# Layer 0's inverse roots of the first groups: from GpSimd's power operation to VectorE's Newton steps

## What is computed

```python
h = layernorm(x) * (1 + ca) + sa
x = x + ga * attn(h)         # attn ends: out = (out - mu) * rsqrt(var + EPS) * ln_w + ln_b; u * out @ Wout.T + bout
h = layernorm(x) * (1 + cb) + sb
# expert layer: two of 8 experts for each token, in the order of the tokens, at most 640 tokens for each expert
gate_logits = xt @ Wg + bg;  top_v, top_i = top_k(gate_logits, 2)
expert_label = one_hot(top_i, E).sum(axis=1)
seq = cumsum(expert_label, axis=0) * expert_label      # the place of a token in its expert's queue
flat_idx = where((seq > 0) & (seq <= capacity), e * capacity + seq - 1, E * capacity)
buf = zeros((E * capacity + 1, d)).at[flat_idx.reshape(-1)].set(src)
```

## Time and profile before

| | us |
|---|---|
| median of 3 runs | 839.18 (839.06 to 839.41) |
| the profiled execution | 838.07 |
| its span, first to last instruction | 836.7 |
| PE busy | 799.2 (96%) |
| DVE busy | 604.1 (72%) |
| ACT busy | 434.5 (52%) |
| POOL busy | 395.0 (47%) |
| chain that ended last | PE 72%, POOL 9%, DVE 6%, issue 5%, DMA 4%, ACT 3% |

### The profile page before, as it was taken

One profiled execution on the slowest core, in us unless ns is written; L12 is line 12 of the kernel. 1 busy time (PEld: TensorE's weight loads), 2 busy tenths in 40 slices (PEclk: granted clock), 3 DMA queues, 4 the chain that ended last, 5 costly groups with the idle time before them and its releaser, 6 DMA issues.

```text
span 836.7 us, 32664 instructions
## 1 busy us (share of the span) xinstructions
PE 799.2 (96%) x13828; PEld 699.4 (84%) x13828; DVE 604.1 (72%) x1779; ACT 434.5 (52%) x942; POOL 395.0 (47%) x399
## 2 busy tenths in 40 slices
PE   6999987899998899999999999999999999989998
PEld 5777767799997688888888888888898889878887
DVE  7898887567545766675777776786867777768865
ACT  6556634344544746566566565575665654523322
POOL 4348887425454735643646646447443434400000
PEclk9999999999999999999999999999999999999999
DMA  9814141233413000000100000200000000048751
GB/s 282 285 45 181 41 134 26 76 94 116 131 48 110 27 3 4 28 4 4 53 4 4 29 4 3 55 4 3 4 3 4 4 4 3 3 87 158 150 117 38
DMA packets 67904, 49.66 MB, mean 59 GB/s; under 512 B 5343, under 2 KB 62774, under 8 KB 67376
## 3 DMA queue, kind: packets, MB, share of 16 engines
q1 hardware_dynamic: 64288, 42.41, 18.8%
q0 software_dynamic: 3328, 5.16, 1.9%
q10 hardware_dynamic: 144, 0.02, 0.0%
HBM read 33.20 MB, written 16.10 MB: 59 GB/s over the span
## 4 chain that ended last, share of the span: by engine, by line
PE 72%; POOL 9%; DVE 6%; issue 5%; DMA 4%; ACT 3%; SPq 1%; DVEq 0%; POOLq 0%; ACTq 0%
PE psum L1625 16%; POOL disp L312 7%; PE psum L1730 7%; PE psum L1755 7%; PE psum L1781 7%; PE psum L2421 5%; PE psum L1299 5%; PE psum L1692 5%; PE psum L2439 4%; PE psum L1770 4%; PE psum L1672 3%; PE psum L1644 3%; PE psum L1335 3%; POOL sb_l_y L231 2%; DMA sb_e_x<-disp 1%
## 5 line engine op out<-in xcount | busy, mean ns | idle before, releaser
L2320 POOL TENSOR_TENSOR sb_a_qr<-sb_h,sb_a_csq 128x512 f32<-128x512 f32 x64 | 81.0, 1287 | 92.1 <-PE psum L1755 88.2
L1625 PE MATMUL psum<-sb_wkv,sb_a_hs 128*128 128x512 f32 (+1 forms) x414 | 122.1, 407 | 1.0 <-ACT sb_a_hs L2108 0.7
L2320 POOL TENSOR_TENSOR sb_a_qr<-sb_a_qp,sb_a_csq 128x512 f32<-128x512 f32 (+1 forms) x64 | 72.2, 1150 | 94.9 <-PE psum L1755 94.9
L1916 ACT ACTIVATE sb_a_vr<-sb_a_va,sb_consts 128x520 f32<-128x520 f32 x128 | 86.6, 726 | 14.4 <-DVE sb_a_va L2178 14.1
L312 POOL DMA_INDIRECT disp<-sb_h,sb_slot x64 | 68.4, 1069 | 23.4 <-issue 18.1
L1625 PEld LDWEIGHTS psum<-sb_wkv,sb_a_hs 128*128 128x128 f32 x414 | 66.0, 190 | 12.5 <-ACT sb_a_hs L2108 0.9
L1730 PE MATMUL psum<-sb_a_mid,sb_a_qr 64*64 64x65 f32 x2048 | 70.6, 218 | 0.0
L1755 PE MATMUL psum<-sb_a_vr,sb_a_kb 64*64 64x130 f32 x1920 | 70.5, 272 | 0.0
L2199 DVE TENSOR_TENSOR sb_a_mid<-psum,sb_a_state 128x130 f32<-128x130 f32 x112 | 47.3, 422 | 26.5 <-PE psum L1755 26.4
L1229 POOL DMA_INDIRECT chosen<-sb_m_h3t,sb_e_row x40 | 39.3, 983 | 57.1 <-ACTq L1413 42.4
L2178 DVE TENSOR_TENSOR sb_a_va<-psum,sb_rows 128x512 f32<-128x512 f32 x64 | 44.0, 688 | 30.6 <-PE psum L1625 30.6
(11 more groups left out here) (292 smaller groups left out, 1983.1 us busy)
## 6 DMA issues: line engine op xcount, KB each, us to landing
sb_h<-turned SPq DMA_DIRECT2D x32, 256.0 KB, 5.5
sb_e_w<-in_w SPq DMA_DIRECT2D x24, 256.0 KB, 3.2
chosen<-sb_empty SPq DMA_DIRECT2D x8, 512.0 KB, 6.4
sb_a_g<-chosen SPq DMA_DIRECT2D x12, 256.0 KB, 3.3
disp<-sb_empty SPq DMA_DIRECT2D x4, 650.0 KB, 9.9
sb_e_x<-disp SPq DMA_DIRECT2D x7, 325.0 KB, 5.0
sb_a_wo<-in_wo SPq DMA_DIRECT2D x4, 512.0 KB, 4.2
out<-sb_x SPq DMA_DIRECT2D x7, 256.0 KB, 3.9
```

Of the source, the lines that this page charges most:

```text
L1625: ins = self.pe.matmul(out[:, x * w:(x + 1) * w], stationary, moving[:, x * w:(x + 1) * w], start=(k == 0 and x == 0), stop=(k == 2), skip ...
L1916: ins = act.activation(self.Vr[i % 2][:, :, k, :], self.Va[i % 3][:], ACT.Copy, scale=self.c[("cos1", "sin1")[k]][:, n:n + 1])
L2320: ins = g.tensor_tensor(self.Qr[i % 2][:, k, :, t], qp, rows(self.csQ[:, k, c * P + t.start:(c + 1) * P], PH), ALU.mult)
```

## The change

Two GpSimd calls of the loop go away: the output roots of rounds 0 to 5 and the input roots of groups 0 to 4. That is 11 power operations; the joint ones after the loop stay. GpSimd's list in the loop is then only its sends, and in the first two rounds the keys roots. The three Newton steps of `last_root` become a helper, `newton_root`, with 11 instructions on 128 x 4 elements, and VectorE calls it for these 11 roots too:

- the input root of group `c` at the start of round `g = c + 1`, with nothing woven in, and `input_means(c)` directly behind it, so that `outputs_gated(g)` now comes after both;
- the output root of group `g` where the labels were, woven with the labels of group `g - 1`. In round 0 there are no labels, and it stands alone.

```diff
     def l0_gpsimd(self):
...
         for it in range(NGRP - 2):
-            if it:
-                self.input_roots(it - 1)
             self.dispatch(3, it - 2)
-            self.output_roots(it)
             if it < 2:
                 self.keys_roots(3 + 2 * it)
...
-    def last_root(self, between):
...
+    def input_root(self, c, between):
+
+        self.dve.wait_ge(self.S["ln3"], c + 1)
+        self.dve.wait_ge(self.S["l0_xn3"], c)
+        self.newton_root(self.t3[:], self.y3[:], between).then_inc(self.S["l0_root3"], 1)
+
+    def output_newton(self, g, between):
+
+        self.dve.wait_ge(self.S["l0_ve"], g + 1)
+        self.dve.wait_ge(self.S["l0_x"], g)
+        self.newton_root(self.t2[:], self.y2[:], between).then_inc(self.S["l0_root2"], 1)
+
+    def newton_root(self, t, y, between):
+
+        v, vs, h = self.dve, self.vs, self.h3[:]
         v.tensor_scalar(h, t, -0.5, None, ALU.mult)
         k = vs.did(v.tensor_scalar(y.bitcast(I32), t.bitcast(I32), -0.5, MAGIC, ALU.mult, ALU.add))
         for n in range(3):
-            next(between)
+            next(between, None)
             v.wait_ge(vs.sem, k)
             k = vs.did(v.tensor_tensor(t, y, y, ALU.mult))
...
     def l0_vector(self):
...
             if g < 2:
                 self.keys_stats(3 + 2 * g)
+            if c >= 0:
+                self.input_root(c, iter(()))
+                self.input_means(c)
             self.outputs_gated(g)
-            if c >= 0:
-                self.input_means(c)
             self.keys_rotated(a)
...
             if c >= 0:
                 self.input_gated(c)
-                self.route_labels(c)
+            labels = self.label_parts(c) if c >= 0 else iter(())
+            self.output_newton(g, labels)
+            for _ in labels:
+                pass
...
-        self.last_root(labels)
+        self.input_root(NGRP - 1, labels)
```

More of the change, by code:

```diff
@@ L274, in output_gates @@
             g.tensor_tensor(self.wog[k][:], rows(self.scaled[k][:], B), gate, ALU.mult).then_inc(S["l0_wog"], 1)
-    def output_roots(self, g):
-        S = self.S
-        self.pool.wait_ge(S["l0_ve"], g + 1)
-        self.pool.wait_ge(S["l0_x"], g)
-        self.inverse_root(self.y2[:], self.t2[:]).then_inc(S["l0_root2"], 1)
-    def input_roots(self, c):
-        S = self.S
-        self.pool.wait_ge(S["ln3"], c + 1)
-        self.pool.wait_ge(S["l0_xn3"], c)
-        self.inverse_root(self.y3[:], self.t3[:]).then_inc(S["l0_root3"], 1)
     def joint_roots(self, c):
@@ L949, in input_stats @@
                        ).then_inc(S["ln3"], 1)
-    def last_root(self, between):
-        v, S, vs, t, y, h = self.dve, self.S, self.vs, self.t3[:], self.y3[:], self.h3[:]
-        v.wait_ge(S["ln3"], NGRP)
-        v.wait_ge(S["l0_xn3"], NGRP - 1)
+    def input_root(self, c, between):
[8 more added lines that the diff above has]
+        v, vs, h = self.dve, self.vs, self.h3[:]
         v.tensor_scalar(h, t, -0.5, None, ALU.mult)
@@ L969, in last_root @@
                 k = vs.did(ins)
-        ins.then_inc(S["l0_root3"], 1)
+        return ins
     def last_normed(self):
```

## The result

| | before | after |
|---|---|---|
| median, same chip, 6 runs each | 839.29 | 851.11 |
| ratio, 95% interval | | 1.0147 (1.0122 to 1.0173) |
| the profiled execution | 838.07 | 851.8 |
| its span | 836.7 | 850.5 |
| mean granted clock | 0.996 | 0.982 |

What follows compares the result with a forecast made beforehand. The prediction took a ring through VectorE, GpSimd's roots, ScalarE and TensorE to bound the loop, and GpSimd the tail. Root costs of 6.9 us plus 1.1 for the clock, 8.0, on 839.18 gave 847.2 us, range 844.0 to 849.8.

Steps and rivals of the forecast that it cites:

- GpSimd's roots gave nothing: Loop: without its 11 roots GpSimd only idles; removal gives at most 0.8 us while the last slots keep their time.
- Bare root 1.98 us: VectorE, rounds 0 and 1: a root with nothing woven in, dependent steps 0.19 us apart, costs 1.98 us.
- Woven root 0.44 us: VectorE, rounds 1 to 5: an output root among the labels adds 0.44 us, bounds 0.3 and 0.7.
- The sum of 6.9 us: Rounds 0 to 5: the root costs on VectorE's and TensorE's path add to 6.9 us, without the clock.
- TensorE's path has no slack from an even round to the next: Rounds 2 to 3 and 4 to 5: labels 0.44 us later make TensorE's L522 0.44 us later, +0.88 in all.
- a shorter way from L848 to L986 gives nothing back there: Rounds 2 to 3 and 4 to 5: statistics to input means falls from 2.61 to 2.18 us without paying for the root.
- `ou` behind L986, nothing added: Gated outputs after the input means: 0.7 us more VectorE work fits in 4.66 us; at worst 0.2 us in four rounds.
- The clock, 1.1 us: TensorE, round 1: idling over 4 us before L512 lowers the clock; costs 1.1 us, bounds 0 and 1.7.
- a rival at 10%: Rounds 2 and 4: 2.0 us idle lowers TensorE's clock again, two more losses of 1.7 us, 850.6 us; chance 10%.
- the range for 8 in 10: Whole program: time between 844.0 and 849.8 us, a little wider than the forecast's own 845.0 to 849.0.
- Successive logits in rounds 1 to 5 15.3, 13.7, 15.3, 13.7 us apart: Sign in the profile after: successive L987 that far apart, where a round was 14.05 or 13.25 us.
- Everything behind layer 0 starts later by that amount: After layer 0: all is TensorE's own work, so the 8.0 us delay carries to the end, nothing given back.

Runs made afterwards that it cites:

- the dummies: Changed kernel with 11 power operations put back on GpSimd on a scratch tile, waited for by nobody; ratio 1.0160 on chip 7.
- the filled kernel: Changed kernel with all sends after the loop and nine wide spare TensorE products in rounds 1, 2 and 4; variances of group 6 at 122.09 us.
- before without its sends: Kernel before with all of GpSimd's sends made after the loop; variances of group 6 at 115.24 us.
- the filled kernels: Changed kernel, sends kept, with spare TensorE products in rounds 1, 2 and 4: 31 narrow, ratio 1.0753 on chip 8; nine wide, 1.0569 on chip 14.
- after without sends: Changed kernel with all of GpSimd's sends made after the loop; variances of group 6 at 126.64 us on chip 0, 126.42 on chip 3.
- products in round 1 only: Changed kernel with 19 spare TensorE products before the output product of round 1 alone; ratio 1.0693 on chip 7.
- woven version: Against before, only input roots of groups 1 to 4 moved to VectorE, woven with the slots at the round's end; ratio 1.0069 on chip 14, 0.9985 on chip 3.
- input roots only: Against before, only the input roots moved to VectorE, bare, ahead of the gated outputs; output roots stay on GpSimd; ratio 1.0056 on chip 14.
- the fillers: Changed kernel with spare TensorE products ahead of the wait for gated outputs, in round 1 or in rounds 1, 2 and 4; ratios 1.0764, 1.0693, 1.0753, 1.0569.
- the one with the first roots given back: Changed kernel with the output root of round 0 and the input root of group 0 back on GpSimd; ratio 1.0258 on chip 7.
- output roots only: Against before, only the output roots moved to VectorE, bare; input roots stay on GpSimd; ratio 1.0101.

## Why the prediction was off by 3.9 us

- *GpSimd's roots gave nothing*: right. GpSimd idles at least 4.7 us before each group, and no cost of the dummies is seen.
- *Bare root 1.98 us*: 2.14 in round 0, from 39.19 to the reader at 41.33, and 2.04 in round 1, from 48.75 to 50.79. The steps are 0.195 each, about the 0.19 of the earlier trace rows; the last one, to the reader of round 0, is 0.31. The Trainium skill's sentence in VectorE: DVE Perf Modes, section The DRAIN you can't avoid, that the semaphore costs nothing extra, is not borne out for these operations on 128x4: they stand 0.195 us apart where they wait for each other and 0.07 to 0.08 where they don't. No run has the same chain without its waits.
- *Woven root 0.44 us*: 0.35 on VectorE by the row, and the steps of the filled kernel into rounds 3 and 5, which carry nothing else, were 0.37 and 0.38.
- *The sum of 6.9 us*: measured 6.85, and right to 0.1 us round by round. Small misses cancel in it: the bare roots are 0.06 to 0.16 us longer than priced and the woven ones 0.07 to 0.09 shorter. It includes the two readings that looked least safe, that TensorE's path has no slack from an even round to the next, and that a shorter way from L848 to L986 gives nothing back there; before without its sends shows both.
- *`ou` behind L986, nothing added*: right with the clock at full.
- *The clock, 1.1 us*: this step failed. It was counted once. In round 1 it cost 1.78 on chip 0, just above the upper bound of 1.7 and well above the 1.1 taken: the fall lasted on while TensorE worked, 0.50 up to 56 us, and all its work from L497 to L520 lies on the path. Against the filled kernels, the same fall cost 1.6 us on chip 8 and 3.0 on chip 14. And the clock fell again in rounds 2 and 4, 1.37 and 1.40 us more on chip 0. The prediction had this as a rival at 10%, with 2.0 us of idle time (measured 1.86 and 1.64) and 850.6 us in all. The measured 851.1 is that rival. Its chance was set low without a reason from the rows, and only with so low a chance could the range for 8 in 10 stop at 849.8. The trace of before had a nearer row. The fall to 0.57 from 137 to 141 us came soon after a gap of only 1.70 us, the row below, and a second one of 0.87 us. With that row, falls in rounds 2 and 4 had to be called at least as likely as not. In the runs most gaps of 1.6 to 1.9 us brought a fall, and three passed without one.

```profile
134.85 0.41 PE L544 MATMUL psum<-sb_rt_label,sb_consts 128*128 128x32 f32 x2 [1.70 <-DVE sb_rt_label L1030]
```

- *Successive logits in rounds 1 to 5 15.3, 13.7, 15.3, 13.7 us apart*: measured 16.93, 13.54, 16.95, 13.55. The two that were right are the ones without a fall.
- *Everything behind layer 0 starts later by that amount*: right within 0.5 us. It is 12.0 us at the first joint root, 12.5 at the last send, 12.2 in the experts of the first layer and 11.8 over the medians. The 13.8 at the end of the profiled execution hold the fall at 767 us. The tail's own low stretch is longer than before (148 to 158 us against 137 to 141), and the experts behind it start no later for it.

## What to carry to other kernels

When a serial piece is moved in front of an instruction that feeds TensorE, price two things: the piece, by the distance between two dependent instructions of that size in the trace, and each idle gap that it makes on TensorE, as a possible fall of the clock. Here they cost 6.9 and 4.6 us, though two of the three gaps were under 2 us. Such a short gap is a chance and not a certainty, so give each its own chance and let the range reach to the sum with all of them. Price a ring of engines round by round and compare the shift summed up so far; filling TensorE's gaps then separates the two parts. As a remedy rather than a test, a filler has to be timed as a whole, since its price may come due in another layer.

## What the runs showed of the hardware

**Short gaps and the clock.** The same idle time of TensorE before the output product went both ways. Among others, the clock fell after 1.86 and 1.64 us (after), 1.63 and 1.58 (after without sends, chip 0), 1.95 (products in round 1 only) and 1.33 (woven version, chip 3). It stayed at 1.00 after 1.85 and 1.62 us (input roots only), 1.63 (after without sends, chip 3, round 2) and 1.34 (woven version, chip 14). The idle times of 2.5 to 5.1 us in round 1 all brought a fall. What decides between two equal gaps, no run shows.

**Late products on some chips.** On chips 7, 8 and 14 readers of TensorE's products start up to 6 us after the last product should be done, in most rounds of after. After on chip 8, round 3: TensorE turns the tokens, and then ScalarE modulates them, which waits for nothing but these four turns and earlier work:

```profile
88.82 0.60 PE L507 MATMUL psum<-sb_consts,sb_xn 128*128 128x128 f32 x4
```
```profile
94.96 0.78 ACT L708 ACTIVATE sb_h_t<-psum,sb_mt 128x512 f32<-128x512 f32 x1 [5.29 <-remote]
```

The turns would end at 89.4 and their reader starts 5.5 us later; the granted clock reads 1.00 up to 92 us. The waits of this kind, for before and for after on chip 8 (total us, times, longest):

```profile
ACT sb_h_t L723 <- remote: 3.9, 2, 2.0
```
```profile
ACT sb_h_t L708 <- remote: 20.1, 4, 5.3
```

Neither kernel has such a wait in its loop on the first chip. With them the logits of after are 20 to 21 us apart in rounds 2 to 5, and its ratio is 1.031 and 1.035 instead of 1.015. The kernels that had some 5 us of it in most rounds (after, the fillers, the one with the first roots given back) are those in which GpSimd only sends in the later rounds. Those that kept a root on it in each round waited mostly 0.4 to 2.2 us, but output roots only had 4.1 us once and the woven version 4.3 once. The runs meant to decide whether the sends are the cause were on chips without late products, so the cause stays open.

**Dependent small operations.** VectorE's 128x4 operations each last 0.15 to 0.17 us by their rows and start 0.195 us apart in a chain, so eleven of them cost 2.0 to 2.1 us bare. Woven between the labels, where others fill the waits, they cost 0.35 us.
